# Where a cross-attention and mixture-of-experts kernel splits its gate/up weights and biases into fp16 halves

## The reference

```python
x = x + xattn(layernorm(x), ctx, W_qkv, W_out, b_out)
x = x + ffn(layernorm(x), Wg, bg, Wgu, bgu, Wd, bd)

# ffn, for every token
logits = xt @ Wg.T + bg
top_vals, top_idx = top_k(logits, 2); rw = softmax(top_vals)
gu = xt @ Wgu[e] + bgu[e]           # gate = even columns, up = odd columns
gate = minimum(gate, 7); up = clip(up, -7, 7)
gated = (up + 1) * gate * sigmoid(1.702 * gate)
out = sum over the two experts of rw * (gated @ Wd[e] + bd[e])
```

## Time and profile before

| what | value |
| --- | --- |
| median of 3 runs | 602.51 us (600.73 to 603.49) |
| span of the profiled execution | 636.7 us |
| busy, PE / DVE / ACT / POOL | 542.6 / 519.7 / 484.4 / 450.0 us |
| pair 15, from its first `nbias` to that of pair 16 | 416.39 to 441.78 us |
| pairs 16 and 17, up to the first block load | 441.78 to 470.78 us |
| expert blocks and the end | 470.78 to 636.7 us |

### The profile page before, as it was taken

One profiled execution on the slowest core, in us unless ns is written; L12 is line 12 of the kernel. 1 busy time (PEld: TensorE's weight loads), 2 busy tenths in 40 slices (PEclk: granted clock), 3 DMA queues, 4 the chain that ended last, 5 costly groups with the idle time before them and its releaser, 6 DMA issues.

```text
span 636.7 us, 20049 instructions
## 1 busy us (share of the span) xinstructions
PE 542.6 (85%) x6760; PEld 457.3 (72%) x6760; DVE 519.7 (82%) x1482; ACT 484.4 (76%) x1366; POOL 450.0 (71%) x555
## 2 busy tenths in 40 slices
PE   2899999999999999999999999977778687778700
PEld 1578898988999889889898899876435565556500
DVE  5879999999999999999999999988756456465516
ACT  1899999999999999999999999978425445455410
POOL 8996585988989889889898898753533455545530
PEclk9999999999999999999999999999789879898755
DMA  9772383174062947228337407550122332221139
GB/s 258 222 274 53 59 287 68 46 261 124 19 185 72 308 132 248 60 57 302 81 55 267 125 12 221 175 119 3 28 62 70 82 82 66 69 69 56 33 115 302
DMA packets 69701, 81.63 MB, mean 128 GB/s; under 512 B 8116, under 2 KB 47564, under 8 KB 69604
## 3 DMA queue, kind: packets, MB, share of 16 engines
q1 hardware_dynamic: 56244, 67.60, 36.8%
q0 software_dynamic: 4352, 8.47, 4.0%
q10 hardware_dynamic: 9008, 4.30, 2.5%
HBM read 18.82 MB, written 46.31 MB: 102 GB/s over the span
## 4 chain that ended last, share of the span: by engine, by line
PE 66%; DVE 9%; issue 7%; ACT 7%; DMA 3%; ACTq 2%; another core or an unknown queue 2%; POOL 2%; SPq 0%; POOLq 0%
PE bank L1258 15%; PE bank L1259 15%; PE bank L1260 15%; PE bank L1378 8%; PE bank L1430 5%; PE bank L1466 3%; DMA ctx_sb<-results 2%; ACT probs L564 2%; PE bank L1497 1%; PE bank L1524 1%; ACTq L462 1%; POOL results L833 1%; DVE pT L1071 1%; ACT pT L576 1%
## 5 line engine op out<-in xcount | busy, mean ns | idle before, releaser
L564 ACT ACTIVATE probs<-bank,nbias 128x128 f32<-128x128 f32 x512 | 146.4, 369 | 4.2
L833 POOL DMA_INDIRECT results<-z,stage x72 | 71.0, 986 | 73.3 <-ACT z L618 53.0
L1071 DVE TENSOR_TENSOR pT<-bank,pT 128x512 f16<-128x512 f32 x128 | 87.6, 684 | 10.9 <-ACT pT L576 7.8
L1050 DVE TENSOR_REDUCE qmax<-bank 128x4 f32<-128x512 f32 x128 | 87.1, 680 | 2.0 <-remote 1.4
L1260 PE MATMUL bank<-keys,q_pad 128*128 128x128 f16 x480 | 86.7, 219 | 0.3 <-issue 0.3
L1259 PE MATMUL bank<-keys,q_pad 128*128 128x128 f16 x480 | 86.6, 219 | 0.0
L1258 PE MATMUL bank<-keys,q_pad 128*128 128x128 f16 x480 | 86.6, 219 | 0.0
L576 ACT ACTIVATE pT<-bank 128x512 f16<-128x512 f32 x128 | 78.2, 611 | 7.2 <-PE bank L1378 4.6
L1378 PE MATMUL bank<-ident,probs 128*128 128x128 f32 x512 | 78.4, 276 | 5.5 <-DVE pT L1071 2.9
L770 POOL DMA_INDIRECT places<-payload,slots x64 | 65.3, 1020 | 16.3 <-issue 11.8
L1258 PE MATMUL bank<-xT,w_qkv 128*128 128x256 f16 x256 | 69.9, 273 | 1.1 <-DVE xT L879 0.8
(11 more groups left out here) (261 smaller groups left out, 2015.5 us busy)
## 6 DMA issues: line engine op xcount, KB each, us to landing
places<-z SPq DMA_DIRECT2D x8, 4160.0 KB
q_pad<-q_nat SPq DMA_DIRECT2D x120, 128.0 KB, 2.4
stage<-places SPq DMA_DIRECT2D x64, 65.0 KB
ctx_sb<-results SPq DMA_DIRECT2D x14, 256.0 KB, 5.0
ctx_sb<-in_ctx_dram ACTq DMA_DIRECT2D x4, 512.0 KB, 10.6
stage<-in_L_ffn_Wgu_dram SPq DMA_DIRECT2D x1, 2048.0 KB, 9.5
out_dram<-x_sb ACTq DMA_DIRECT2D x7, 256.0 KB, 5.5
stage<-in_L_xattn_W_qkv_dram SPq DMA_DIRECT2D x3, 512.0 KB, 6.6
```

The costliest lines, as they stand in the source:

```text
L564: last = nc.scalar.activation(probs[:, b, k, :], score_bank[b][:, k * P:(k + 1) * P], ACT.Exp, bias=nbias[:, b, k:k + 1], scale=exp_scale)
L833: nc.gpsimd.indirect_dma_start(out=results, out_offset=bass.IndirectOffsetOnAxis(ap=to, axis=0), in_=z[:, (q - 5) % NZ, t, :], in_offset=None,
L1050: nc.vector.tensor_reduce(qmax[:, r % 2, :], score_bank[r % 2][:, :].rearrange("p (h k) -> p h k", h=4), AX.X, ALU.max).then_inc(s["qmax_o ...
L1071: nc.vector.tensor_tensor(pT[:, r % 2, LO, :], pt_bank[:, :], pT[:, r % 2, HI, :], ALU.subtract).then_inc(s["pt_lo"], 1)
```

## The change

The two tables become one: part `k` is split in step (15, k), its high half on ScalarE and its low half on VectorE. `split_biases` moves from step (16, 6) to step (15, 2). The two low halves behind the table of blocks go away there. No instruction is added or removed, and what is computed is the same.

```diff
-        GU_HIGH = {(15, 1): (0,), (15, 4): (1,), (15, 7): (2,), (16, 3): (3,), (16, 4): (4,), (16, 5): (5,), (17, 3): (6, 7)}
-        GU_LOW = {(15, 1): (0,), (15, 4): (1,), (15, 7): (2,), (16, 6): (3, 4), (16, 7): (5,)}
+        GU_AT = {(15, r): (r,) for r in range(8)}
...
-                for k in GU_HIGH.get((p, r), ()):
+                for k in GU_AT.get((p, r), ()):
...
-                if (p, r) == (PAIRS, 6):
+                if (p, r) == (PAIRS - 1, 2):
                     split_biases()
...
-                for k in GU_LOW.get((p, r), ()):
+                for k in GU_AT.get((p, r), ()):
                     gate_up_low(k)
...
-            gate_up_low(6)
-            gate_up_low(7)
```

## The result

The changed kernel takes 605.87 us (605.07 to 606.77, 5 runs) against 602.51 us: a ratio of 1.0059, with a 95% interval of 1.0044 to 1.0073, so 3.4 us or 0.6% slower. That is inside the stated range of 601.6 to 607.2. It is also just above 605.5, from which the prediction counted a change as slower (chance 0.34); the interval reaches from 0.44 to 0.73% and so holds that 0.5%. That pair 15 pays for VectorE's new work is what was forecast. But the sum was 1.0 us short, and its parts are off by more than that, so that the agreement is in part luck; how that came about teaches more than the agreement.

What follows compares the result with a forecast made beforehand. No engine was idle enough to be free, and VectorE had almost no room in pair 15. 2.8 us added there less 0.35 us from the drain gave +2.4 us, so 604.9 us, with a range of 601.6 to 607.2.

Steps and rivals of the forecast that it cites:

- Pair 15 is bound by VectorE, and pays for what is put into it: Pair 15: VectorE, busy 13.74 of 14.67 us in steps 3 to 7, passes 2.8 us of new work on.
- Step 0 costs nothing: Pair 15, step 0: the new part's 0.66 us goes into idle time in step 2; otherwise up to 0.7 us.
- The gap that was to take it up: Pair 15, step 2: idle time with unnamed releaser, 1.44 us on VectorE and 2.31 us on ScalarE.
- Step 2 delays by 1.45 us, steps 3 and 5 by 0.66 each, step 6 by nothing: Pair 15: delays reaching pair 16 from VectorE's added low halves and, in step 2, the biases; sum 2.8 us.
- The pieces only delay, at their own length: Pair 15: added VectorE pieces, 0.66 us a low half and 1.23 us of biases, delay by length less idle time.
- The drain gives back 0.35 us: Pairs 16 and 17: without low halves beside it, GpSimd's `shift` shortens, so `slots` and the last scatters come 0.35 us earlier.
- the drain is bound by VectorE: Rival, drain: the chain's 3.4 us come back whole and pair 15 hides all but 0.3: 599.4 us, chance 0.08.
- Low halves 6 and 7, SyncE and the transfers are hidden: Behind the table of blocks: removing or moving this work saves nothing, at most a tenth or two from the transfers.
- GpSimd is held up in pair 15: Rival, pair 15, step 6: the low half holds up `rstd` and `shift` for 0.66 us: 605.6 us, chance 0.12.
- Both engines pay: Rival, pair 15: ScalarE's 3.3 us can't overlap VectorE's, or the unnamed gap is absent; 4.5 us arrive: 606.7, chance 0.15.
- Nothing of the delay arrives: Rival, pair 16: ScalarE's 2.71 us wait for an unnamed releaser swallows the 2.8 us late start: 602.2 us, chance 0.15.
- the forecast length of pair 15: Pair 15, from its first `nbias` to that of pair 16: 28.2 us in place of 25.4.

Runs made afterwards that it cites:

- ScalarE's halves alone: Kernel before with all eight of ScalarE's high halves in the steps of pair 15, VectorE's low halves and biases unmoved: 603.33 us, ratio 1.0018.
- the profile with the biases taken out: Changed kernel with the biases split in step (16, 6) again instead of (15, 2): 605.29 us, ratio 1.0035.
- the fills: Changed kernel plus seven filling matmuls on TensorE in step (15, 3), computing nothing needed: 606.28 us, ratio 1.0051; repeated, 606.63 us, ratio 1.0055.
- the disturbed execution: The first profile of the unedited kernel before, on which the prediction was built: span 636.7 us beside a median of 602.5 us.
- the second profile: The kernel before profiled again without an edit: span 601.4 us, 603.12 us for this one execution.
- the last: The unedited changed kernel timed again in the last series, beside the kernel before and one with filling matmuls: 607.80 us, ratio 1.0081.

## Why the prediction was nearly right, point by point

- **Pair 15 is bound by VectorE, and pays for what is put into it.** Right over the whole pair: ScalarE's halves alone cost 0.64 us, all ten halves 2.5, halves and biases 5.1. Not right step by step: in steps 0, 2 and 6 the next `nbias` comes as late with ScalarE's halves alone (0.64, 0.52, 0.65 us) as with all ten (0.63, 0.49, 0.64). VectorE's low halves alone were not run.
- **Step 0 costs nothing.** Wrong, 0.63 us, and by ScalarE's high half. The gap that was to take it up was not the kernel's; the same holds for ScalarE's wait in step 2. In the prediction I named 0.7 us for the case that the gap isn't there, and should have taken the timed runs as a warning: a profile 34 us above the median has waits that they haven't.
- **Step 2 delays by 1.45 us, steps 3 and 5 by 0.66 each, step 6 by nothing.** Neither the sum nor the places were right. The profile with the biases taken out gives, by step from `nbias` to `nbias`, +0.63, 0, +0.49, +0.17, 0, +0.24, +0.64, +0.33: 2.5 us for the halves. The biases add 1.4 (26.85 less 25.48, both at full clock in that pair). So even without any fall of the clock my 2.8 stands against 3.9: step 0 adds 0.6, steps 6 and 7, which I took as nothing, 1.0 together, and step 2 with the biases 0.4 (0.49 + 1.37 against 1.45), while steps 3 and 5 came out 0.5 and 0.4 smaller than forecast.
- **The pieces only delay, at their own length.** This is the step that failed, and with steps 0, 6 and 7 the cause of the short sum. The delay of VectorE leaves TensorE idle for 2.1 us, its clock falls to the lower level around its return, and this costs 0.5 to 1.3 us more (27.40, 27.93 and 28.12 us against 26.85 with the fills). I had named the clock at the end as something that could go wrong, without a price.
- **The drain gives back 0.35 us.** Nearly right. `mv` to logits went from 4.84 to 4.51 us, 0.33 less by `shift` (0.50 to 0.19 us), against the 3.4 us that the chain of waits seemed to promise; to the last scatter it was 0.16, from 11.99 to 11.83. The rival that the drain is bound by VectorE is out.
- **Low halves 6 and 7, SyncE and the transfers are hidden.** Right. From the last scatter to the first block's rows it takes 5.8 us before and 5.7 to 6.1 after.
- **GpSimd is held up in pair 15.** This rival came true beside the forecast, with less than its 0.66 us. In the changed kernel `rstd` lies under the low half of step 6 (439.83 to 440.57 us):

```profile
439.68 0.22 POOL L671 TENSOR_SCALAR var_eps<-mv 128x2 f32<-128x2 f32 x1 [14.74 <-DVE mv L1101]
439.98 1.18 POOL L673 TENSOR_TENSOR rstd<-var_eps,minus_half 128x2 f32<-128x2 f32 x1
```

It takes 1.18 us; in the kernel before and in that with ScalarE's halves alone, 0.73 and 0.72. ScalarE's wait for `shift` ahead of `y` grows with it, from 0.48 to 0.91 us, and step 7 by 0.33. The Trainium skill's rule ("SBUF — State Buffer", section "Who interferes with whom": a VectorE instruction with two SBUF inputs and a GpSimd instruction that reads SBUF exclude each other) fits all four places: this one, `shift` in the drain, and `var_eps` and `rstd` in the kernel with only the biases moved.

- **Both engines pay, 606.7 us.** I gave it a chance of 0.15. One of its two conditions came true: the unnamed gap isn't there in an undisturbed execution. In the profile 5.1 us arrive, 3.9 of them at full clock, less 0.3 in the drain; that is nearer to its 4.5 than to my 2.8. The two engines' halves don't add up, though: ten halves cost 2.5 us, not 3.3 twice.
- **Nothing of the delay arrives.** Out. All of it reaches pair 16, whose length stays at 11.3 us where the clock doesn't fall. The 2.71 us of unnamed wait in pair 16 was of the disturbed execution; in the second profile the longest wait of ScalarE there is 1.53 us, for TensorE.

The sum of the changed profile's stretches is larger than the change of the time: +5.1 us in pair 15 and +4.2 from pair 15's start to the end, against +3.4 in the first measurement and +4.8 (603.04 to 607.80 us) in the last. The ratio of the last, 1.0081, would make 607.4 us of the first's 602.51, just outside the stated range. The last stretch, 131.5 to 133.4 us in these profiles, varies by more than a microsecond in either kind of kernel, and the clock falls at some place in many executions. What makes the first measurement a microsecond lower than the stretches is left open.

That the forecast length of pair 15, 28.2 us, came true (28.1) was luck: it was 2.8 us on top of a stretch that held 2.4 us of a stall that the undisturbed profile hasn't. The pair grew by 5.1 us, which lies outside the bounds of 1.5 to 4.5 us that I had put on it; even the case in which nothing on VectorE is hidden was too small, since it had no price for the clock.

## What to carry to other kernels

A chain of waits that runs over an instruction doesn't say that it would be shorter without it: look at what the next instruction on the chain waits for besides (here the logits' product ended 0.04 us before), and at what hides the work where it would go. A delay put on one engine of a tight loop is not worth its own length alone, since an engine that it leaves idle may come back slower. And before a sum is built on a profiled execution, hold its span against the timed runs: a gap with an unnamed releaser in a profile that is 34 us too long is no place to hide work in.
